# Count lists moved from the plan block into the attend block, and block ends without POOL drains

## The reference

```python
edge_index = jnp.stack([src, dst])
x = x + _L0_gnn_ref(_layernorm(x), W, attn_l, attn_r, bias, src, dst)
x = x + _L0_ffn_ref(_layernorm(x)[None], ...)[0]          # 8 experts, top 1
x = x + _L1_gnn_ref(_layernorm(x), edge_index, ...)       # two graph convolutions
x = x + _L1_ffn_ref(_layernorm(x)[None], ...)[0]          # 8 experts, top 2

def _L0_gnn_ref(h, W, attn_l, attn_r, bias, src, dst):    # N, H, D = 6250, 4, 64
    feat = (h @ W).reshape(N, H, D)
    el = jnp.einsum('nhd,hd->nh', feat, attn_l)
    er = jnp.einsum('nhd,hd->nh', feat, attn_r)
    e = jax.nn.leaky_relu(el[src] + er[dst], 0.2)
    ex = jnp.exp(e - segment_max(e, dst)[dst])
    alpha = ex / segment_sum(ex, dst)[dst]
    rst = segment_sum(feat[src] * alpha[..., None], dst) + bias
    return h + jax.nn.elu(rst.reshape(N, H * D))
```

## Time and profile before

| | |
|---|---|
| median of 3 runs | 5529.09 us (5528.75 to 5536.25) |
| profiled execution, its own time | 5532.8 us |
| its span | 5531.0 us |
| plan block ends, projection begins | near 149 us |
| attend block | near 233 to 2496 us |
| POOL busy, L740 | 1715.6 us in 1664 gathers |

### The profile page before, as it was taken

The page is one execution under the profiler, slowest core; times in us unless marked ns, Lnnn a source line. Parts: engine busy times, 40 slices in busy tenths (PEclk is TensorE's granted clock), DMA queues, the critical chain, the costliest instruction groups (busy, mean ns, idle before and its releaser), DMA issues. The chain is left out here.

```text
span 5531.0 us, 113538 instructions
## 1 busy us (share of the span) xinstructions
PE 4370.6 (79%) x23328; PEld 3442.3 (62%) x23329; DVE 3274.5 (59%) x10456; ACT 2973.3 (54%) x7576; POOL 2196.6 (40%) x2057
## 2 busy tenths in 40 slices
PE   2566555656888888884799699998999973699999
PEld 1444332324666666663799577776777753699998
DVE  7699776667999999997455533335333355222222
ACT  0325666666777777776233356665566656233332
POOL 2477777776777777772222000000000006222222
PEclk9799887777999999995899899999999985899999
DMA  4367888887888888884566266773444454566665
GB/s 134 114 208 255 273 284 282 293 286 243 237 235 235 237 234 238 237 229 125 161 179 176 81 191 215 224 222 110 118 133 134 133 156 141 157 179 181 181 182 144
DMA packets 623476, 1075.06 MB, mean 194 GB/s; under 512 B 77344, under 2 KB 501993, under 8 KB 616648
## 3 DMA queue, kind: packets, MB, share of 16 engines
q1 hardware_dynamic: 503992, 727.33, 43.0%
q0 software_dynamic: 112144, 265.80, 18.1%
q10 hardware_dynamic: 7200, 80.28, 3.7%
HBM read 775.81 MB, written 303.15 MB: 195 GB/s over the span
## 5 line engine op out<-in xcount | busy, mean ns | idle before, releaser
L740 POOL DMA_INDIRECT arena<-table,arena x1664 | 1715.6, 1031 | 531.2 <-issue 446.8
L1416 PE MATMUL banks<-parts,a_wide 128*128 128x512 f32 x4900 | 1178.4, 399 | 18.0 <-ACT a_wide L1439 18.0
L1416 PEld LDWEIGHTS banks<-parts,a_wide 128*128 128x128 f32 x4900 | 917.0, 189 | 262.3 <-ACT a_wide L1439 46.8
L940 PE MATMUL banks<-arena 128*128 128x261 f32 x3328 | 938.2, 406 | 0.0
L686 PE MATMUL banks<-arena 128*128 128x392 bf16 x2368 | 602.2, 407 | 411.2 <-ACT banks L714 228.1
L1439 ACT CAST a_wide<-arena 128x896 fp32r<-128x896 f16 x700 | 659.0, 942 | 420.3 <-PE banks L1416 405.4
L2347 ACT ACTIVATE rings<-banks,b_sb 128x128 f32<-128x128 f32 x1296 | 370.6, 369 | 828.3 <-PE banks L2380 828.2
L2164 POOL DMA_INDIRECT expert_in<-arena,slot x147 | 160.7, 1093 | 1647.3 <-DVEq L2109 1605.6
L686 PEld LDWEIGHTS banks<-arena 128*128 128x128 bf16 x2368 | 338.0, 149 | 674.9 <-issue 632.4
L2380 PEld LDWEIGHTS banks<-yt_ring,arena 128*128 128x128 f32 x5184 | 609.1, 193 | 15.5 <-DVE yt_ring L2269 4.4
L2380 PE MATMUL banks<-yt_ring,arena 128*128 128x128 f32 x5184 | 610.4, 276 | 6.2 <-DMA arena<-in_L_ffn_W 2.2
(11 more groups left out here) (368 smaller groups left out, 5583.4 us busy)
## 6 DMA issues: line engine op xcount, KB each, us to landing
arena<-counts SPq DMA_DIRECT2D x700, 224.0 KB, 2.5
arena<-in_L_ffn_W SPq DMA_DIRECT2D x114, 1024.0 KB, 10.0
edge_rows<-arena SPq DMA_DIRECT2D x364, 264.0 KB, 3.3
arena<-edge_rows SPq DMA_DIRECT2D x364, 264.0 KB
counts<-arena ACTq DMA_DIRECT2D x50, 1568.0 KB
arena<-in_L_ffn_w SPq DMA_DIRECT2D x64, 1024.0 KB, 8.6
arena<-near_rows SPq DMA_DIRECT2D x416, 128.0 KB
expert_in<-rings SPq DMA_DIRECT2D x25, 2028.0 KB
```

What stands on the lines that cost most here:

```text
L740: pool.indirect_dma_start(out=got[:, r, j, :], out_offset=None, in_=table0, in_offset=bass.IndirectOffsetOnAxis(ap=src_sb[:, 2 * pair + j: ...
L940: last = pe.matmul(banks_a[u][:, 0:mw], onehot[:, u % GS, j, :], msg[:, u % RB, j, 0:mw], start=False, stop=False, skip_group_check=True)
L1416: last = pe.matmul(psum[u][:, 0:2 * D], a_wide[:, at:at + P], parts[:, a * 2 * D:(a + 1) * 2 * D], start=(a == 0), stop=(a == NT - 1))
```

## The change

It has four parts.

1. The count lists leave the plan block. The two list loads go to SP's part of the projection, after the weights, the eight iotas to POOL's part of it, and `count_dve` and `count_pe` to the attend block, between the peaks and the keys. The row statistics of x stay in the plan block.
2. `fetch_pairs` leaves POOL's part of the projection. It now stands in POOL's row of kept pairs, after 22 of them, and waits there for `cidx` and for PE's last list product; the key making waits for its gathers.
3. SP no longer waits for the plan block's stores before it loads the weights, but at the projection's end. The source of zeros and one iota move to the place of a later buffer (`a_wide`).
4. Kept pair n waits until the fill has done (n - 64) x 592 / 364 groups (`LEAD`), and every block is made with `no_gpsimd_drain=True`.

The fill itself stays as it is, with two units of four banks.

```diff
+LEAD = 64
+LISTS_AT = 22
...
-        with nc.Block() as block:
+        with nc.Block(no_gpsimd_drain=True) as block:
...
-            def count_sp(sp):
+            def count_loads(sp):
                     sp.dma_start(last_i...).then_inc(in_, 16)
                     sp.dma_start(th_i...).then_inc(in_, 16)
+            def count_landed(sp):
+                    sp.wait_ge(in_, 32)
-            def count_dve(dve):
+            def count_dve(dve, v_, pe_):
...
-                    for t in range(NT):
-                        dve.bn_stats(stats[:, t:t + 1, :], xres[:, t, :]).then_inc(k_stats, 1)
-                    first_stats(dve)
...
             def count_rows(pool):
+                    pool.wait_ge(q_rows, 16 * len(row_cuts))
+                    pool.wait_ge(q_zero, 16 * len(zcuts))
...
-            def fetch_pairs(pool):
-                    pool.wait_ge(q_rows, 16 * len(row_cuts))
+            def fetch_pairs(pool, v_, pe_, g_):
+                    pool.wait_ge(v_, mark["cidx"])
+                    pool.wait_ge(pe_, 4)
                     for k in range(BK):
...
-                    pool.wait_ge(g_, 32 * BK)
...
                 def cook_dve(dve):
+                    dve.wait_ge(l_g, 32 * BK)
...
                         for n in range(NKEPT):
+                            if n == LISTS_AT:
+                                fetch_pairs(pool, l_v, l_pe, l_g)
                             wait(pool, s_st[r], 16 * turn)
+                            wait(pool, done, (n - LEAD) * (BP // PG) // NKEPT)
                             fetch(pool, r, pair_of(i, KEPT[k]), s_keep[r])
...
                         peaks["vector"](dve)
+                        count_dve(dve, l_v, l_pe)
                         cook_dve(dve)
...
                         peaks["tensor"](pe)
+                        count_pe(pe, l_v, l_pe)
                         cook_pe(pe)
...
         def load_gat(sp, s):
-            sp.wait_ge(q_zero, 16 * len(zcuts))
-            sp.wait_ge(q_o, 32)
-            sp.wait_ge(q_rows, 16 * len(row_cuts))
             sp.dma_start(wraw, ...).then_inc(s, 16)
...
+            sp.wait_ge(q_rows, 16 * len(row_cuts))
+            count_loads(sp)
+        def gat_settle(sp):
+            count_landed(sp)
+            sp.wait_ge(q_o, 32)
```

More of the change, by code:

```diff
@@ L254, in build @@
         assert used[0] <= wgcn_at
+        wide_at = -(-nc.sbuf_base // 32) * 32
         a_wide = sb("a_wide", [P, 2 * CW], F32R)
         seen = sb("seen", [P, 2, 2 * D], F32R)
+        assert BCOL <= 2 * CW + 4 * D and TB * D <= 2 * CW
+        piota_row = nc.alloc_sbuf_tensor_at("piota_row", [P, BCOL], F32, offset=wide_at).ap()
+        zeros = piota_row[:, 0:TB * D]
         centre, total, squares = (rings[:, n * D:(n + 1) * D] for n in range(3))
@@ L296, in own @@
             return a[:, bass.ds(v, 1)]
-        k_c, k_x, k_pad, k_stats = sem("k_c"), sem("k_x"), sem("k_pad"), sem("k_stats")
-        with nc.Block() as block:
+        k_c, k_pad, k_stats = sem("k_c"), sem("k_pad"), sem("k_stats")
+        k_x = [sem(f"k_x{t}") for t in range(0, NT, 8)]
+        with nc.Block(no_gpsimd_drain=True) as block:
             @block.gpsimd
@@ L438, in height @@
                 return min(P, NW - g * P)
-            in_, c_, v_, pe_, g_ = (sem("count_" + n) for n in ("in", "c", "v", "pe", "g"))
+            in_, c_ = sem("count_in"), sem("count_c")
             mark = {}
@@ L990, in _ @@
                         walk_act(act)
-            return count_sp, count_rows, count_dve, count_pe, fetch_pairs, attend
+            return count_loads, count_landed, count_rows, attend
         last_i = acc_flat[0:1, 0:NBP].bitcast(I32)
@@ L1024, in build @@
         zero_to = expert_flat[0:P * zspan].rearrange("(p c) -> p c", p=P)
-        count_sp, count_rows, count_dve, count_pe, fetch_pairs, attend_and_count = count_plan()
-        with nc.Block() as block:
+        count_loads, count_landed, count_rows, attend_and_count = count_plan()
+        with nc.Block(no_gpsimd_drain=True) as block:
             @block.sync
@@ L1135, in _ @@
                 listed["q_v"] = link.n
-                count_dve(dve)
+                for t in range(NT):
+                    if t % 8 == 0:
+                        dve.wait_ge(k_x[t // 8], 16)
+                    dve.bn_stats(stats[:, t:t + 1, :], xres[:, t, :]).then_inc(k_stats, 1)
+                first_stats(dve)
                 dve.wait_ge(q_g, 16 * 2 * PCH)
@@ L1215, in _, with project @@
                     act.activation(t_a, var, ACT.Sqrt, bias=eps[:, 0:1]).then_inc(s_sq, 1)
-        def project(tag, width, w_sb, rows_of, evac, load, n_load, before=None, n_before=0, store=None, gather=None):
+        def project(tag, width, w_sb, rows_of, evac, load, n_load, before=None, n_before=0, store=None, settle=None, number_rows=None):
             s = {n: sem(tag + "_" + n) for n in ("w", "y", "t", "yt", "f", "e", "b", "q", "h", "n")}
             s["out"] = [sem(f"{tag}_out{u}") for u in range(TB)]
-            with nc.Block() as block:
+            with nc.Block(no_gpsimd_drain=True) as block:
                 @block.sync
@@ L1228, in _ @@
                             sp.wait_ge(s["out"][u], 16 * NG)
-                if gather:
+                        settle(sp)
+                if number_rows:
                     @block.gpsimd
                     def _(pool):
-                        gather(pool)
+                        number_rows(pool)
                 def groups(eng, body):
@@ L1711, in build @@
                 {"act": gat_out_act, "dve": gat_out_dve}, load_gat, 48, before=build_gat, n_before=9,
-                store=gat_store, gather=fetch_pairs)
+                store=gat_store, settle=gat_settle, number_rows=count_rows)
         reuse_semaphores()
```

32 lines of the change are left out of this document (13 added, 19 removed).

## The result

The changed kernel took 5567.9 us (median of 4 runs, 5565.6 to 5570.1), the kernel before 5531.1 us (4 runs, 5528.8 to 5536.3): 1.0062 times as long, with a 95% interval of 1.0048 to 1.0076 (the two medians alone give 1.0066). That is 36.8 us slower between the medians, where 43 were forecast.

A forecast was written before the change was run, and what follows sets the result against it. Two clocks start the walk: the chain through DVE to the fill's end, and POOL's stream. Terms -68.3, -4, +127.9, +4, +1 give +60.6; -17.2 for drains leaves +43.4, forecast 5572 us, range 5540 to 5595.

The forecast's parts named there:

- The chain: First attention layer: plan, projection, lists, list gathers and keys in series put the first one-hot 60.6 us later, at 338.8.
- Its two largest terms: Attend block, in front of the keys: 73.4 us of count lists and 54.5 us of list gathers, together 127.9.
- The plan block: Count lists leave, row statistics follow at 50.1 and end at 67.8: the block shrinks by 68.3 us.
- The load of the projection: SP asks for weights without waiting for the column stores: -4 us; list DMAs behind them covered by the queue.
- The +4: Attend block: list products at a lower granted clock could grow by 0 to 12.6 us, taken as +4.
- The +1: Attend block: DVE's list operations may hold a gather or two, 0 to 5 us, taken as +1.
- The drains: POOL's drain goes at block ends: -3.4 and -7.7 us at two serve blocks, -6.1 at the program's end.
- The zero for the first expert block: End of first expert block: POOL clears semaphores with every engine waiting, so dropping the drain gains nothing (0 to -4).
- The fill: Attend block: same instructions, banks and ring, so its length stays 1015 us, with 1% either way.
- A: Attend block: POOL is the limit and the fill gives way, so faster, 5500 us; chance 0.12.
- B: Attend block: POOL, held by DVE's list operations, comes 20 us late to the lists, 5592 us; chance 0.08.
- C: Block ends: the drains are not worth anything, so +60.6 us, 5590 us; chance 0.10.

The follow-up runs named there:

- Experiments 3 and 4: List gathers heading POOL's attend block in the kernel before: 5580.1 us; changed kernel with 0 or 45 kept pairs ahead of them: 5570.8 and 5613.5 us.
- experiment 6: Small list loads moved: in old_order behind x's loads or onto ACT's plan-block queue, in the changed kernel onto ACT's projection queue: 5509.2, 5508.1, 5566.9 us.
- old_order: The kernel before without GpSimd's drains, SP's waits moved from ahead of the projection's weight loads to behind its table stores: 5514.0 us, ratio 0.9957.
- loads_last: The changed kernel with the two small list loads issued at the projection's end instead of right behind its weights: 5570.2 us, ratio 1.0057.
- gathers_only: The kernel before with only POOL's list gathers moved to the head of its attend block, lists still in the plan block: 5580.1 us, ratio 1.0087.
- Experiments 1 and 2: The kernel before without GpSimd's drains: 5511.8 us, ratio 0.9955; the changed kernel with the drains put back: 5588.5 us, ratio 1.0097.
- lists_at_0: The changed kernel with the list gathers ahead of all kept pairs, 0 instead of 22 pairs before them: 5570.8 us, ratio 1.0071.
- lists_at_45: The changed kernel with 45 instead of 22 kept pairs ahead of the list gathers: 5613.5 us in one run.
- no_drain: The kernel before with GpSimd's drain left out at all nine block ends, nothing else changed: 5511.8 us, ratio 0.9955.

## Why the prediction was right, and where it was not

**The chain, right.** The time is set by plan, projection, lists, list gathers, keys, one behind the other, and fill and walk follow. Its two largest terms, 73.4 and 54.5, were measured as 73.4 and 52.2. The second was too large: the last gather landed 2.95 us after its issue (301.14 to 304.09) and not 7.2, the median of the DMA view, which was taken beside the projection's own transfers. 1.2 us of slower issuing and 0.8 us between the last product and the first gather took part of that back. Experiments 3 and 4 show the same chain from two more sides.

**The plan block, 5 us too small.** "After the change the statistics follow at 50.1" took the start from the trace of before and overlooked that a load stood in front of it that goes too. The 1666 small pieces held up DVE's first load; experiment 6 gets the same 5 us (25.81 to 20.60) in the old order.

**The load of the projection, the wrong sign.** The forecast gave -4 for the waits and "nothing" for the list DMAs, since the queue covered them. The waits were worth some 1.2 (old_order), and the list DMAs cost 4.4 to 5.4 (loads_last). Between old_order's 8.5 us and loads_last's 7.0 stand 1.5 more: POOL's gathers no longer run beside the load, and gathers_only, without them, has 9.1 against 9.6 and 9.8, so they may be half of it; the rest is open. Together with the plan block it is one term that the forecast did not have: 5 us of stalled DMA that were moved from one block into another. By chance the two errors nearly cancel.

**Low clock and held gathers.** The +4 was 0: the products did not slow at 0.69 (19.18 us against 19.13), and the forecast names no row for the factor of 1.66 from which it was taken; no run here shows one for these products. The +1 was about right: the list gathers that DVE held are the 1.2 us of slower issuing. Those held ahead of them, beside the lists, ate into POOL's wait and cost nothing.

**The drains, 5 us too small.** 3.4, 7.7 and 6.1 were 3.5, 6.4 and 6.9 in the changed kernel. The zero for the first expert block was wrong: "every engine waiting" is the very case in which the drain is paid. The drain there takes 4.63 us. Experiments 1 and 2 give 21.5 and 24 us in profiles, 24 and 19 to 21 in times, against 17.2.

**The fill, right within its range**, and the walk behind it: their sum moved by 2.7 us, and in the thirteen profiles it lies between 2217 and 2226 us. That is wider than the 2.7, so neither the +9.2 nor the -6.6 can be told from no effect of the change. What the forecast is off by, 6 us, is 5.5 on the way to the first one-hot and 5 on the drains, less some 4 of scatter behind it.

**What was to be seen**, foreseen and found: plan block over near 81 and at 75.5; first attend gather near 170 and at 171.5; DVE's hole some 45 us and 40.3; first one-hot near 339 and at 333.3; ACT's copies over near 1353 and at 1356.2; POOL still for some 70 us and for 75.4.

**Rivals.** A (POOL is the limit): lists_at_0 and gathers_only delay POOL's kept pairs by 55 and 48 us and the fill takes no notice. What spoke for it, POOL and fill ending within 12 us of each other, was two independent streams that happened to meet. B: real (lists_at_45), with 11 us to spare. C: out.

**A version that beats both.** The old order without drains: 5511.8, 5514.0, 5509.2 and 5508.1 us in four forms, 0.43 to 0.48% below the kernel before and 1% below the changed one. So the moved lists only cost time, and the gain is the drains'. The last two also have the small pieces out of the way; what that adds is within the scatter of the times, though it is seen in the profiles (the plan block is 131.4 and 131.9 us long instead of 133.9 and 134.1).

## What to carry to other kernels

Work that stands in an idle engine's time beside a load is not free to move: before moving it, write down which resource each of its parts waits for at the new place, and add up what then stands in series. Two streams that end at nearly the same time need not bound each other; shift one on purpose by some tens of microseconds and see whether the other follows. And where a wait on a load does not fit the bytes that are in flight, look for a transfer of many small pieces near it, on any queue.

## What the hardware showed

- Two loads of 1568 and 98 pieces of 4 bytes (6.7 KB) held what stood in the same queue up by 4.4 to 5.4 us, and by as much with a queue of their own in the projection, by some 3 with one in the plan block; other data moved at 20 to 32 GB/s meanwhile. Alone at the end of a block they took 7 to 8 us from issue to the block's end, 5.1 of them with idle DMA engines. Where they are held was not tried: the 1568 all go to one partition.
- POOL's drain at the end of the four blocks that end on scatters took 4.05 to 8.06 us, and under 0.3 us in the block ends where POOL had been idle. Where the other engines were done, leaving it out made the block 3.6 to 6.7 us shorter (no_drain).
- The lists' products (of one column, of one row by 512, and small transposes) took the same time at a mean clock of 0.69 as at 1.00 (19.18 and 19.13 us for 182).
- Beside a TENSOR_SCALAR of 128 x 2432 from float32 to bf16 a gather took 2.58 to 2.74 us of POOL instead of 0.95, and 7.39 us beside a TENSOR_TENSOR of 98 x 6400 that takes 6.83.
